# Moving z's products of in_proj behind the last FFN product in a fused Mamba and FFN kernel

## The reference, cut to what matters

```python
x1 = x + layernorm(mamba(layernorm(x)))      # x: 2 sequences x 2048 tokens x 256
out = x1 + layernorm(ffn(layernorm(x1)))

def mamba(x):
    h = rmsnorm(x) * norm_w
    u, z = split(h @ in_proj.T)               # 512 + 512 channels
    uc = silu(conv4(u) + conv_b)
    dt, B, C = split(uc @ x_proj.T)
    dt = softplus(dt @ dt_proj.T + dt_b)
    for n in range(16):                       # 16 states; a scan over tokens for each
        h_n[t] = exp(dt * A_n)[t] * h_n[t-1] + (dt * B_n * uc)[t]
        y += h_n * C_n
    y = (y + uc * D) * silu(z)
    return y @ out_proj.T + x

def ffn(x):                                   # ternary weights, 256 -> 1024 -> 1024 -> 1024 -> 256
    h = silu(x @ w1) * (x @ w2)
    return gelu(gelu(h @ h1) @ h2) @ w3
```

## Time and profile before

| | us |
|---|---|
| median of 3 runs (lowest, highest) | 1510.74 (1508.67, 1510.95) |
| the profiled execution | 1509.34 |
| its span, first to last instruction | 1507.6 |
| busy: PE, DVE, ACT, POOL | 1310.3, 1308.9, 1199.0, 1135.0 |
| mean granted TensorE clock | 0.929 of full speed |

### The profile page before, as it was taken

The page is one execution under the profiler, slowest core; times in us unless marked ns, Lnnn a source line. Parts: engine busy times, 40 slices in busy tenths (PEclk is TensorE's granted clock), DMA queues, the critical chain, the costliest instruction groups (busy, mean ns, idle before and its releaser), DMA issues.

```text
span 1507.6 us, 27022 instructions
## 1 busy us (share of the span) xinstructions
PE 1310.3 (87%) x9264; PEld 1191.4 (79%) x9264; DVE 1308.9 (87%) x1993; ACT 1199.0 (80%) x2605; POOL 1135.0 (75%) x1351
## 2 busy tenths in 40 slices
PE   6565799898989989898998989899998989898897
PEld 4243689797978979797888879788887979787797
DVE  6999998998989899898989889898989989897842
ACT  6555688888888889888888888888888888887753
POOL 4646678878878787887878888787888888777620
PEclk8576799999999999999999999999999999998999
DMA  7400111111101111110111111011111111010000
GB/s 275 145 22 23 42 29 32 41 34 37 37 23 44 31 44 34 37 38 20 44 37 38 37 38 38 20 41 36 38 37 37 38 29 39 23 45 23 30 4 17
DMA packets 39169, 63.21 MB, mean 42 GB/s; under 512 B 5249, under 2 KB 19457, under 8 KB 38929
## 3 DMA queue, kind: packets, MB, share of 16 engines
q10 hardware_dynamic: 18944, 33.83, 7.3%
q1 hardware_dynamic: 19984, 26.02, 5.4%
HBM read 55.38 MB, written 4.46 MB: 40 GB/s over the span
## 4 chain that ended last, share of the span: by engine, by line
PE 30%; DVE 29%; ACT 27%; issue 9%; POOL 3%; DMA 1%; SPq 0%; ACTq 0%; DVEq 0%; POOLq 0%
DVE S L1723 10%; DVE acc L1737 7%; PE fP L785 6%; PE fP L786 6%; ACT dA L1304 5%; PE sT L809 4%; DVE hP L1757 4%; PE fP L773 3%; ACT Rw L1497 2%; PE hP L773 2%; PE hP L952 2%; ACT Rw L1432 2%; POOL Glo L661 2%; DVE fP L1792 2%; ACT hP L1384 2%
## 5 line engine op out<-in xcount | busy, mean ns | idle before, releaser
L591 POOL TENSOR_TENSOR S<-X,Bs 128x1024 f32<-128x1024 f32 x255 | 609.8, 2391 | 153.3 <-PE sT L809 117.5
L1723 DVE TENSOR_TENSOR_SCAN S<-dA,S 128x512 f32<-128x512 f32 x512 | 620.4, 1212 | 55.9 <-POOL S L594 26.3
L1304 ACT ACTIVATE dA<-delta,A 128x255 f32<-128x255 f32 x1024 | 444.2, 468 | 214.1 <-DVE S L1723 213.6
L809 PE MATMUL sT<-ident,S 128*128 128x128 f32 x2048 | 323.9, 285 | 82.1 <-DVE acc L1737 78.1
L785 PE MATMUL fP<-Ghi,w_h 128*128 128x256 f32 x1512 | 381.0, 291 | 0.4 <-ACT Rw L1491 0.4
L786 PE MATMUL fP<-Glo,w_h 128*128 128x256 f32 x1512 | 364.2, 280 | 0.0
L1737 DVE SCALAR_TENSOR_TENSOR acc<-sT,CT,acc 128x512 f32<-128x512 f32 x480 | 347.2, 726 | 14.9 <-PE sT L809 14.9
L809 PEld LDWEIGHTS sT<-ident,S 128*128 128x128 f32 x2048 | 244.9, 146 | 124.6 <-DVE S L1723 62.2
L785 PEld LDWEIGHTS fP<-Ghi,w_h 128*128 128x128 f32 x1512 | 284.8, 188 | 6.3 <-ACT Rw L1491 4.3
L786 PEld LDWEIGHTS fP<-Glo,w_h 128*128 128x128 f32 x1512 | 284.9, 188 | 0.0
L661 POOL TENSOR_TENSOR Glo<-Rw,Ghi 128x1024 fp32r<-128x1024 f32 x86 | 203.3, 2371 | 74.4 <-ACT Ghi L1503 52.0
(11 more groups left out here) (280 smaller groups left out, 2425.2 us busy)
## 6 DMA issues: line engine op xcount, KB each, us to landing
Bs<-b_rows ACTq DMA_DIRECT2D x128, 256.0 KB, 3.2
xh<-in_x SPq DMA_DIRECT2D x16, 256.0 KB, 2.8
xt<-in_x SPq DMA_DIRECT2D x16, 256.0 KB, 3.2
out<-x SPq DMA_DIRECT2D x15, 256.0 KB, 2.2
Rw<-in_w SPq DMA_DIRECT2D x4, 512.0 KB, 4.4
Rw<-in_h SPq DMA_DIRECT2D x4, 512.0 KB, 6.0
delta<-in_h SPq DMA_DIRECT2D x3, 512.0 KB, 4.4
X<-in_h SPq DMA_DIRECT2D x3, 512.0 KB, 7.2
```

The costliest lines, as they stand in the source:

```text
L591: pool.tensor_tensor(s[:, :, :], X[par][:, :, :], row[:, None, :].broadcast_to([P, DT, T]), ALU.mult).then_inc(scan_pool.sem, 1)
L809: mm = pe.transpose(sT[t][:, d * P:(d + 1) * P], S[slot(third, n)][:, d, t * P:(t + 1) * P], ident[:, :])
L1304: a = act.activation(dA[half][:, i, 1:], delta[par][:, d, 1:], ACT.Exp, scale=A[:, d * N + n:d * N + n + 1])
L1723: a = dve.tensor_tensor_scan(pair, dA[half][:, :, :].rearrange("p d t -> p (d t)"), pair, 0.0, ALU.mult, ALU.add)
```

## The change

1. **z's products.** Only u's two pairs of products are left in half steps 12 and 13, with no wait for z. z's two pairs stand in half steps 17 and 18 and go to the `fP` pair of banks (`bank_z`; for chunk 1 both to `fP[1]`). `USES` gets z0, z1 between a3 and b2; b2 and b3 move from half step 17 to 18, behind z1, and wait for z's readers.
2. **SiLU of z.** DVE's copies are gone. ACT takes the SiLU straight from PSUM in two instructions, at the front of `silus`.
3. **X\*B of state 8.** On POOL, the first remainder of the second hidden layer moves from half step 12 to 13, and both stand behind X\*B of state 8 instead of before it.
4. **`last_product`.** For each half of the tokens all Ghi products come first, each half of them as soon as ACT has cast it, and then the Glo products.
5. **Half step 3.** The Ghi products of h2_0 and h2_1 stand together, then h2_0's Glo products, `out`, and h2_1's Glo products.
6. ACT casts `hi1_1` in half step 1, not 0.

```diff
@@ PE, head_step
-                if 10 <= hs < 14:
-                    q = hs - 10
+                if hs in (12, 13):
+                    q = hs - 12
                     if q == 0:
                         pe.wait_ge(head_act.sem, head_act.at(h, "hT"))
-                    elif q >= 2:
-                        pe.wait_ge(head_vec.sem, head_vec.at(h, ("z0", "z1")[q - 2]))
                     for d in range(2):
-                        m = (2 * q + d + DT) % (2 * DT)
+                        m = 2 * q + d
                         mm = products(hP[(q + 1) % 2][:, d, :], lambda k: w_in[:, k, m * P:(m + 1) * P],
                                       lambda k: hT[:, k, :], KM)
                     mm.then_inc(head_pe.sem, 1)
+                if hs in (17, 18):
+                    q = hs - 17
+                    if h == 1:
+                        if q == 1:
+                            pe.wait_ge(head_act.sem, head_act.at(h, "zs0"))
+                    else:
+                        steps, chunk, name = last_reader(h - 1, f"z{q}")
+                        pe.wait_ge(steps.sem, steps.at(chunk, name))
+                    for d in range(2):
+                        m = DT + 2 * q + d
+                        mm = products(bank_z(h, hp, q)[:, d, :], lambda k: w_in[:, k, m * P:(m + 1) * P],
+                                      lambda k: hT[:, k, :], KM)
+                    mm.then_inc(head_pe.sem, 1)
@@ PE, hidden2_first becomes hidden2_high (both m, Ghi) and hidden2_low (one m, Glo)
                             with pe.Else():
-                                hidden2_first(c - 2, 0)
+                                hidden2_high(c - 2)
+                                hidden2_low(c - 2, 0)
                                 tail_step(c - 1, 1 - par, hs)
-                                hidden2_first(c - 2, 1)
+                                hidden2_low(c - 2, 1)
@@ PE, last_product
                 for t in range(TT):
-                    for k in range(HM):
-                        if t == 0 and k == HM // 2: pe.wait_ge(end_pool.sem, end_pool.at(g, "lo2_1"))
-                        pe.matmul(dst, Ghi[:, k, tok], w_3[:, k, :], start=(k == 0), stop=False)
-                        mm = pe.matmul(dst, Glo[:, k, tok], w_3[:, k, :], start=False, stop=(k == HM - 1))
+                    for half in range(2):
+                        pe.wait_ge(end_act.sem, end_act.at(g, f"hi2_{half}"))
+                        for k in range(half * HM // 2, (half + 1) * HM // 2):
+                            pe.matmul(bank[:, t, :], Ghi[:, k, toks[t]], w_3[:, k, :], start=(k == 0), stop=False)
+                    for half in range(2):
+                        pe.wait_ge(end_pool.sem, end_pool.at(g, f"lo2_{half}"))
+                        for k in range(half * HM // 2, (half + 1) * HM // 2):
+                            mm = pe.matmul(bank[:, t, :], Glo[:, k, toks[t]], w_3[:, k, :],
+                                           start=False, stop=(k == HM - 1))
@@ PE, tail_step
-                parts = {15: (0, (0, 1)), 16: (0, (2, 3)), 17: (1, B_ORDER[:2]), 20: (1, B_ORDER[2:])}
+                parts = {15: (0, (0, 1)), 16: (0, (2, 3)), 18: (1, B_ORDER[:2]), 20: (1, B_ORDER[2:])}
@@ POOL, end_step
-                if hs in (12, 13):
-                    low_part(end_act, g, f"hi2_{hs - 12}", hs - 12).then_inc(end_pool.sem, 1)
+                if hs == 13:
+                    for half in range(2):
+                        low_part(end_act, g, f"hi2_{half}", half).then_inc(end_pool.sem, 1)
@@ ACT, silus
+                if head:
+                    staging_free(h, 6)
+                    act.wait_ge(tail_pe.sem, tail_pe.at(h - 2, "out"))
+                    for q in range(2):
+                        act.wait_ge(head_pe.sem, head_pe.at(h, f"z{q}"))
+                        act.activation(z[hp][:, 2 * q:2 * q + 2, :], bank_z(h, hp, q)[:, :, :],
+                                       ACT.Silu).then_inc(head_act.sem, 1)
...
-                    act.wait_ge(head_vec.sem, head_vec.at(h, "z1"))
-                    act.activation(z[hp][:, :, :], z[hp][:, :, :], ACT.Silu).then_inc(head_act.sem, 1)
@@ DVE, head_step
-                if hs == 12:
...
-                    for q in range(2):
-                        dve.wait_ge(head_pe.sem, head_pe.at(h, f"z{q}"))
-                        dve.tensor_scalar(z[hp][:, 2 * q:2 * q + 2, :], hP[(q + 1) % 2][:, :, :], 1.0, None,
-                                          ALU.mult).then_inc(head_vec.sem, 1)
```

More of the change, by code:

```diff
@@ L323, in build @@
         USES = (["yT0", "yT1", "out"] + [f"h2_{m}" for m in range(2, HM)] + ["xfT", "w3"] + [f"a{i}" for i in range(HM // 2)]
-                + [f"b{i}" for i in B_ORDER] + [f"h1_{m}" for m in range(HM)])
+                + ["z0", "z1"] + [f"b{i}" for i in B_ORDER] + [f"h1_{m}" for m in range(HM)])
         def ring(par, use):
@@ L350, in last_reader @@
                 of_end = USES[at] == "w3" or USES[at].startswith("h2")
-                if end if of_end else tail:
+                of_head = USES[at][0] == "z"
+                if c < CHUNKS - 1 if of_head else end if of_end else tail:
                     return reader(c, USES[at])
@@ L708, in body @@
                         head_factors(h)
-                    if end and hs != 13:
+                    if end:
                         end_step(c - 2, par, hs)
@@ L935, in hidden2, with hidden2_high, hidden2_low @@
                     .then_inc(end_pe.sem, 1)
-            def hidden2_first(g, m):
+            def hidden2_high(g):
                 pe.wait_ge(head_vec.sem, head_vec.at(g + 2, "delta"))
                 pe.wait_ge(tail_act.sem, tail_act.at(g, "hi1_0"))
-                for k in range(HM // 2):
-                    pe.matmul(hP[m][:, 0, :], w_h2[:, k, m * P:(m + 1) * P], Ghi[:, k, :], start=(k == 0), stop=False)
+                for m in range(2):
+                    for k in range(HM // 2):
+                        pe.matmul(hP[m][:, 0, :], w_h2[:, k, m * P:(m + 1) * P], Ghi[:, k, :],
+                                  start=(k == 0), stop=False)
+            def hidden2_low(g, m):
                 pe.wait_ge(end_pool.sem, end_pool.at(g, "lo1_0"))
@@ L976, in last_product @@
-                if stream:
-                    pe.wait_ge(end_piece_used.sem, end_piece_used.at(g, END_PIECES - 1))
-                    mm = pe.nop()
+                bank = ring(gp, "w3")
+                toks = [slice(t * P, (t + 1) * P) for t in range(TT)]
+                if stream:
+                    pe.wait_ge(end_pool.sem, end_pool.at(g, "lo2_1"))
+                    for t in range(TT):
+                        for k in range(HM):
+                            pe.wait_ge(end_piece_in.sem, end_piece_in.piece(g, LAYER_PIECES + t * HM + k))
+                            pe.matmul(bank[:, t, :], Ghi[:, k, toks[t]].bitcast(F32), w_piece[:, :],
+                                      start=(k == 0), stop=False)
+                            pe.matmul(bank[:, t, :], Glo[:, k, toks[t]].bitcast(F32), w_piece[:, :], start=False,
+                                      stop=(k == HM - 1)).then_inc(end_piece_used.sem, 1)
+                    pe.wait_ge(end_piece_used.sem, end_piece_used.at(g, END_PIECES - 1))
+                    pe.nop().then_inc(end_pe.sem, 1)
+                    return
@@ L1071, in body @@
                         end_step(c - 2, par, hs, tail)
+                    if head and hs == 18:
+                        head_step(c + 1, 1 - par, hs)
                     if tail and hs != 3:
                         tail_step(c - 1, 1 - par, hs)
-                    if head:
+                    if head and hs != 18:
                         head_step(c + 1, 1 - par, hs)
@@ L1505, in end_step @@
             def end_step(g, gp, hs):
[L1506 removed]
+                if hs == 1:
                     round_half(g, tail_act, "gelu1_1", 1)
```

29 lines of the change are left out of this document (8 added, 21 removed).

## The result

The changed kernel takes 1576.69 us (median of 4 runs, 1573.99 to 1578.03), the kernel before on the same chip 1510.55: ratio 1.0438, 95% interval 1.0420 to 1.0456. It is 66 us slower; 23 were forecast. The profiled execution has a span of 1573.7 us, and a mean granted clock of 0.903 against 0.929.

The account below looks back on a forecast made before the run. Four nearly equally loaded engines, bound by a chain of waits through ACT, DVE, POOL and PE. 1509.3 - 4.9 + 13 x (2.3 - 0.1) gives 1533.0, plus 1.4 for the runs' median: 1534 us, range 1504 to 1544.

Parts of the forecast that it names:

- The bodies of today: Bodies 2 to 14 before the change: most take 86.5 us; 4.9 us are extra, 3 x 1.2 from bodies 3, 5, 7.
- z's copies, worth 0: DVE's copies of z, 20.5 us in all, gain nothing, since ACT sets the first tap and DVE waits there anyway.
- the sign named for it: DVE's wait before the first tap: over 3 us if the copies gain nothing, under 2 us if they were on the path.
- z's products leave 10 and 11; X\*B of state 8 first: PE runs ahead with nothing waiting; POOL's second remainder ends near 868.4 instead of 867.5, costing 0 at full clock.
- PE's clock, 2.3 us a body: At the last product, PE's idle time halves its clock for about 4.6 us, losing 2.3 us a body, bounds 1.2 and 2.85.
- The falls of the clock near half steps 18 and 24 go: These drops of PE's clock should vanish because z's products fill PE there, and bring nothing.
- hi1_1 and the Ghi products, 0.1: The later cast and h2's Ghi products together remove waits of DVE and PE: gain 0.1 us a body, bounds 0 and 0.45.
- SiLU of z in front, 0: In ACT's SiLU block, DVE waits longer at half step 19 and less at 21: net 0, bound 0.25.
- b2 and b3 behind z's SiLUs: On PE these products wait for z's SiLUs, with state 8's second-half transposes queued behind: cost 0, bound 0.3 us.
- Bodies 0, 1, 15: The bodies at the ends, where waits shift between engines: 0 for the three together, bounds -3 and +3 us.
- The clock does not fall: Rival: PE keeps full clock at the last product, all bodies like body 4, 1504.5 us in the runs; chance 0.12.

Follow-up runs that it names:

- e12: e7 with both copies of u from PSUM done by DVE at half steps 12 and 13 instead of by ACT: 1506.05 us, ratio 0.9980.
- e9: e12 with the last product's first remainder on DVE at half step 14 instead of POOL, fills 7, 3, 1, 3: 1493.86 us, ratio 0.9898.
- e1: The changed kernel with products b2 and b3 behind the transposes of state 8's second half: 1535.34 us, ratio 1.0173.
- e7: The changed kernel with e1's edit and 7, 3, 3 and 4 fill products in the last product's waits: 1502.84 us, ratio 0.9966.
- e6: The changed kernel with 13 products with zeros ahead of the wait for the remainder at half step 24: 1547.45 us, ratio 1.0270.
- e3: The changed kernel with e1's edit and 14, 7, 6 and 8 fill products in the last product's waits: 1524.96 us, ratio 1.0104.
- e4: The kernel before with the move of z alone (products, SiLU from PSUM, b2 and b3 at 18): 1568.67 us, ratio 1.0401.
- e5: The changed kernel without the move of z, all other parts of the change kept: 1543.42 us, ratio 1.0247.

## Why the prediction was wrong

The direction was right and so was the first of two mechanisms; the second, which brought more than half of the loss, was missing: 1534 against 1577, outside the range. Over bodies 2 to 14 the forecast was -4.9 + 13 x 2.2 = +23.7 us, measured +63.2. Step by step:

- *The bodies of today:* the 4.9 us of extra are four bodies, not three and a rest elsewhere. The fourth is body 9 (87.8 us), from which the rows were read, so nine others lose nothing, not ten. Its long stretch at half clock stands at half step 24: the loss that the forecast left out was there once already, 1.3 us.
- *z's copies, worth 0:* right, but the sign named for it was not. One wait of over 3 us before the tap was to show it, and one under 2 us was to show the opposite; the wait is 1.72. The time went into three waits for ACT, in body 9 1.24 (for a decay), 0.87 (for the FFN's input) and 1.72 us, so the reading holds all the same. e12 shows that even 1.1 us less of ACT's work would have brought nothing alone. The Trainium skill, "Perfetto Trace Analysis", section "Identifying the Most-Contended Engine", would have begun with DVE as one of the busiest; here 13 us less of busy time on DVE bought nothing, and a gain came only when work of ACT and POOL was moved to DVE (e9).
- *z's products leave 10 and 11; X\*B of state 8 first:* the second remainder ends 29.4 us into body 9, forecast 29.1. Right.
- *PE's clock, 2.3 us a body:* right in place and size. 20 matmuls at 4.34 us instead of 2.38, the wait at the gather 1.87 (1.5 to 2.5 forecast), 2.40 a body by e1 and e7, about 1.9 in the changed kernel itself. e1 has all of the change but the held transposes; it takes 1535, where I forecast 1534; that it agrees to 1 us is partly luck, since the stretch at half clock is 10.3 us long there and not the 4.6 of the sum. The Trainium skill, "TensorE: Matmul & The Clock Gate", section "HAM oscillation — how this bites in real kernels", said that waits between groups of matmuls let the clock fall anew in each round; the trace agrees, in all of bodies 2 to 14, and in twelve of them at half step 24 as well, which the forecast left out.
- *The falls of the clock near half steps 18 and 24 go:* right at 18, wrong at 24. There three bodies had one before, and twelve have one now.
- *hi1_1 and the Ghi products, 0.1:* e7's bodies are 86.35, 0.15 below 86.5. That fits, but no run has this step alone, so it is not shown.
- *SiLU of z in front, 0:* the wait at half step 19 is 1.87 (1.97 forecast), the next one 0.17 instead of 0.84 and 0.24. Right.
- *b2 and b3 behind z's SiLUs, "0, bound 0.3":* this is the step that failed. The times in it were good: "they come at 884.4, DVE wants them at 886". I asked only who on DVE wants these transposes. But there are three buffers S, so POOL's X\*B of state 11 wants them as well, at 881.2 in the kernel before. It had no wait there, so no row of waits named it. Being 3.3 us late, it moved everything behind it on POOL up to the remainder of half step 24, and PE's gap there, 0.51 us before (0.22 to 1.31 in the other bodies), grew to 3.39. This cost 38.9 us of the 66: 28.9 by the clock and 10.0 directly, by the differences of e1 and e6.
- *Bodies 0, 1, 15:* 0 with a bound of 3; measured +2.9 with what lies around the span's bodies.

The range failed with the same step: its bound of 0.3 us was worked out from one reader. Of the rivals none named a second fall. "The clock does not fall" would have been 1504.5; e7, which is that case with the held transposes mended and fill products added, took 1502.8.

## What to carry to other kernels

When an instruction is put ahead of another on an in-order queue, list everyone who waits for the second, those above all who show no wait today: no row of waits names them, and their slack is in the timeline only. Here the free buffer mattered, not the data. Then follow the delay through the queue of the engine that inherits it to the next gap of PE, and price the gap twice: by its length, and by the half clock behind it. Gaps on PE can be mended by a few products with zeros, as long as they are shorter than the wait; what is beyond it comes back as delay (e3 against e7: 22 us). And an engine's idle time brought something here only when the other engines that tie at its next meeting point were relieved too (e12 against e9: bodies of 86.4 and 85.45 us).

## What the runs showed that I had not expected

- A gap of PE of 3.39 us costs more behind it than in it: with the gap filled and the delay left as it was, 28.9 of 38.9 us came back (e6). In body 14 of the changed kernel the same delay brought no second fall, and the body was 3.9 us shorter.
- The last product lost the clock by either half of the change (e4: idle 3.95 us; e5: 2.06 and 1.58 us), so the halves cost 61 and 36 us alone and 66 together.
- Thirteen products of 128x128 with zeros, in fp32, took 3.07 us (26 records in e6), 0.235 each, and kept the clock: PEclk was 1.00 while they ran and in the 6.1 us behind.
- DVE took 1.22 us for the remainder that takes POOL 2.35.
